# Two instruction groups change places on TensorE and three on VectorE in a batch loop

## The reference

```python
qx = _ln(_fp8_linear_pertensor(ln_out, wqx, ...).reshape(b, s, g, hpg, d), qxln_w, qxln_b)
kvx = einsum('bsi,oi->bso', cond, w_kv_x)          # cond: the context, 8 x 512 x 256
kx, vx = split(kvx, 2, axis=-1)
kx = _ln(kx.reshape(b, sc, g, d), kxln_w, kxln_b)
xout = softmax(einsum(qx, kx) * scale) @ vx
catq = _div_clamp_fp8(concat([core, xout]), proj_smooth)
x = x + einsum(catq, wproj) * (proj_in_scale * proj_w_scale)
```

## Time and profile before

| what | us |
|---|---|
| median of 3 runs | 427.75 (425.83 to 428.95) |
| the profiled execution's own time | 427.4 |
| its span in the trace | 425.6 |
| busy: PE, DVE, ACT, POOL | 414.7, 347.2, 248.8, 35.8 |

### The profile page before, as it was taken

One profiled execution on the slowest core, in us unless ns is written; L12 is line 12 of the kernel. 1 busy time (PEld: TensorE's weight loads), 2 busy tenths in 40 slices (PEclk: granted clock), 3 DMA queues, 4 the chain that ended last, 5 costly groups with the idle time before them and its releaser, 6 DMA issues.

```text
span 425.6 us, 6868 instructions
## 1 busy us (share of the span) xinstructions
PE 414.7 (97%) x2427; PEld 292.2 (69%) x2433; DVE 347.2 (82%) x699; ACT 248.8 (58%) x780; POOL 35.8 (8%) x58
## 2 busy tenths in 40 slices
PE   8999999999999999999999999999999999999897
PEld 3453455788885767778676686785486799837596
DVE  5889999987999899689899998978887787746831
ACT  2478898688547777748986677664505263220220
POOL 0010000040000001100001000010010004101000
PEclk9999999999999999999999999999999999999999
DMA  7599120500002015993554835688337979730000
GB/s 240 226 191 415 39 85 2 199 2 26 27 2 99 1 51 123 201 306 78 132 124 92 198 70 108 155 187 359 74 78 246 390 267 241 151 125 2 2 2 25
DMA packets 14591, 56.80 MB, mean 133 GB/s; under 512 B 1824, under 2 KB 2912, under 8 KB 13280
## 3 DMA queue, kind: packets, MB, share of 16 engines
q1 hardware_dynamic: 11104, 39.31, 25.3%
q0 software_dynamic: 3456, 17.11, 21.4%
HBM read 41.40 MB, written 0.26 MB: 98 GB/s over the span
## 4 chain that ended last, share of the span: by engine, by line
PE 74%; DVE 12%; issue 6%; DMA 4%; ACT 3%; POOL 1%; SPq 0%; DVEq 0%; ACTq 0%; POOLq 0%
PE PS L482 11%; PE PS L1817 10%; PE PS L453 8%; PE PS L454 8%; PE PS L455 8%; PE PS L1846 3%; PE PS L535 3%; PE PS L1287 3%; DMA lutw_dt.float<-luttmp_dt.float 2%; PE PS L1832 2%; DMA raw_dt.float<-in_wk_nat 1%; PE PS L492 1%; PE PS L1153 1%; PE PS L1135 1%; PE PS L1295 1%
## 5 line engine op out<-in xcount | busy, mean ns | idle before, releaser
L605 ACT ACTIVATE sq_dt.float<-PS 128x128 bf16<-128x128 f32 x256 | 67.0, 279 | 27.0 <-PE PS L455 20.5
L482 PE MATMUL PS<-s_dt.float,ctx_ring_dt.float 128*128 128x512 f32 x128 | 57.8, 593 | 0.0
L605 ACT ACTIVATION_READ_ACCUMULATOR sq_dt.float<-PS 128x1 f32 x256 | 53.6, 210 | 0.0
L453 PE MATMUL PS<-wkc_dt.float32r,ctx_hi_dt.float32r 128*128 128x512 f32 x128 | 51.5, 402 | 0.1
L454 PE MATMUL PS<-wkT_dt.float32r,ctx_hi_dt.float32r 128*128 128x512 f32 x128 | 50.0, 390 | 0.0
L455 PE MATMUL PS<-wkc_dt.float32r,ctxT_ring_dt.float32r 128*128 128x512 f32 x128 | 49.9, 390 | 0.0
L687 ACT ACTIVATE luttmp_dt.float<-low_bit_dt.float,vec_dt.float,small_dt.float 128x1536 f32<-128x1536 uint8 x24 | 38.5, 1654 | 8.5 <-DMA lutw_dt.float<-luttmp_dt.float 8.5
L1817 PE MATMUL PS<-wch_dt.float,xs_dt.float 128*128 128x512 f32 x96 | 42.0, 592 | 0.0
L482 PEld LDWEIGHTS PS<-s_dt.float,ctx_ring_dt.float 128*128 128x128 f32 x128 | 23.6, 190 | 23.6 <-issue 23.0
L700 POOL DMA_DIRECT2D lutw_dt.float<-luttmp_dt.float x21 | 18.2, 869 | 234.7 <-DVE luttmp_dt.float L694 234.7
L694 DVE SCALAR_TENSOR_TENSOR luttmp_dt.float<-idx_dt.float,luttmp_dt.float 128x1536 f32<-128x1536 uint8 x21 | 36.6, 1753 | 0.0
(11 more groups left out here) (304 smaller groups left out, 851.3 us busy)
## 6 DMA issues: line engine op xcount, KB each, us to landing
lutw_dt.float<-luttmp_dt.float POOLq DMA_DIRECT2D x21, 768.0 KB, 6.1
wch_dt.float<-in_chunks SPq DMA_DIRECT2D x5, 1024.0 KB, 7.9
ctxT_ring_dt.float<-in_ctxT SPq DMA_DIRECT2D x8, 512.0 KB, 3.4
ctx_ring_dt.float<-in_ctx SPq DMA_DIRECT2D x8, 512.0 KB, 3.9
keysT_dt.float<-in_ctxT SPq DMA_DIRECT2D x8, 512.0 KB, 7.0
keys_dt.float<-in_ctx SPq DMA_DIRECT2D x8, 512.0 KB, 8.0
zu_dt.float<-in_wproj SPq DMA_DIRECT2D x1, 2048.0 KB, 7.2
A_first_dt.float<-in_wproj SPq DMA_DIRECT2D x1, 2048.0 KB, 10.2
```

What stands on the lines that cost most here:

```text
L453: nc.tensor.matmul(o, x_hi, hi[:, c, :], start=c == 0, stop=False)
L482: last = nc.tensor.matmul(mix_bank(b, c), keysr[k][:, t, c * 128:c * 128 + 128], sS[k][:, t, :], start=t == 0, stop=t == KT - 1)
L605: last = nc.scalar.activation(sq[:, (4 * hf + g) * D:(4 * hf + g + 1) * D], key_bank(b, 2 * t + hf)[:, g * D:(g + 1) * D], ACT.Square, acc ...
```

## The change

`total` and `spread` change places on TensorE in the steps 1 to 6. On VectorE `sums` goes ahead of `lo_of_A` (steps 2 to 6; in step 1 `lo_of_A` was behind both already), and the first table term goes from ahead of `shift` to behind `normalise` (steps 1 to 6). Item 7's code is not changed.

```diff
@@ TensorE, step
                 maxima(b)
                 if prev and more:
                     mix(b - 1, 1 - k, 1)
+                    spread(b)
                     total(b - 1)
-                    spread(b)
@@ VectorE, step
+                sums(b - 1, 1 - k)
                 if b > 1:
                     lo_of_A(dve, b + 1)
-                sums(b - 1, 1 - k)
                 maxima(b)
                 if b == 1:
                     lo_of_A(dve, 2)
-                term(dve, b - 1, 0)
                 shift(b, k)
                 normalise(b - 1, 1 - k)
+                term(dve, b - 1, 0)
```

## The result

| | before | the change |
|---|---|---|
| median, 8 runs each in one comparison | 426.87 us (425.83 to 428.95) | 429.70 us (429.00 to 431.13) |
| profiled execution | 427.4 us, span 425.6 | 429.0 us, span 427.2 |

The ratio is 1.0064, 95% interval 1.0044 to 1.0084: slower by 0.6%, which the repeated runs can tell from no change, and within the 1% of the prediction. Forecast were 429.8 us and a loss of 2.05 us.

What follows compares the result with a forecast made beforehand. TensorE's order of work was taken to bound the six changed steps. +1.25 us (step 1) and +0.8 us (step 4) make +2.05 us, 429.8 us against the median 427.75; range 427.0 to 432.0 us, 8 times in 10.

Steps and rivals of the forecast that it cites:

- Step 1: TensorE waits for late maxima before the spread, and its third key product waits through total and ScalarE: +1.25 us.
- Step 4: VectorE has no idle time behind the shift, so TensorE's fourth score product waits 1.35 instead of 0.54 us: +0.8 us.
- The exchange in the other steps: Spread ahead of total on TensorE where maxima are early: zero cost, covered by the mix with 1.09 us margin.
- the sums: Sums ahead of A's low part on VectorE: only margin, maxima about 0.85 us earlier in step 4; no gain in time.
- the normalisation's tie: VectorE's normalisation against ScalarE's Exp of the inverse: margin shrinks from 1.37 to about 0.1 us, priced at nothing.
- The later DMAs: The first term's accumulating DMA, on POOL's queue, is issued some 5 to 6 us later: taken as zero cost.
- The clock: TensorE's clock was forecast to stay 1.00; rival: it falls to 1.2 GHz in step 1, 441.2 us, chance 0.03.
- at most 0.66 us: TensorE's idle time in steps 1 and 4, taken as all a better order could give; faster rival 427.1 us, chance 0.07.
- Steps 3 and 5 are free: VectorE's 0.81 us of lateness fits into idle times of 0.65 and 0.47 us (step 5: 0.63 and 0.46): no cost.
- if a light step grows: Sign that the forecast is wrong: steps 2, 3, 5 and 6 were to stay as long as before.
- VectorE's idle time before each shift: Sign in the changed profile: VectorE idle 1.6 to 1.7 us before each shift.
- The rival of the late leaf: Step 3's third leaf waits for its DMA, delaying the normalisation; at most 2.1 us reach TensorE, 431.9 us; chance 0.15.

Runs made afterwards that it cites:

- the reordering on ScalarE: The change, with ScalarE's split of the context moved ahead of the inverse: 428.40 us, ratio 1.0027 to before.
- The last kernel: Against the change: total ahead of spread in step 1, term in its old place, ScalarE's context split ahead of the inverse; 426.68 us, ratio 0.9980 to before.
- The kernel with the term back in step 4 alone: The change, with total ahead of spread in step 1 and the term ahead of shift in step 4 only: 426.29 us, ratio 0.9982 to before.

## Why the prediction was right

*The sum.* Step 1: forecast +1.25, measured +1.22, and in the two pieces of it that the forecast named: TensorE idle before the spread (0.59 us, released by VectorE's last maxima instruction), and the third key product held through ScalarE. The exchange alone reproduced it, its removal in step 1 took it away, and the reordering on ScalarE took away the part that was said to run through ScalarE. Step 4: forecast +0.8, measured +0.80, wait forecast 1.35 us and measured 1.35 us. The term was its cause, and taking the term back in this step alone gave all of it back.

*Where luck helped.* That 429.8 us came so close to the measured 429.70 is in part luck. The sum stood on a median of 427.75 us from three executions of before, and eight gave 426.87; by medians the loss is 2.8 us (interval 1.9 to 3.6), where 2.05 was forecast. What the forecast got right is its 2.05 against the 2.11 us of the six steps.

*What was priced at nothing.* The exchange in the other steps, the sums and the normalisation's tie were free. The later DMAs cost nothing either: the longest took 11.6 us to land instead of 9.7, and the leaf of step 5 waited 2.00 us instead of 1.98. The clock stayed at 1.00 in every stretch of the profiled execution, over two gaps of 0.6 us in step 1 and one of 1.35 us in step 4. The section on HAM oscillation of "TensorE: Matmul & The Clock Gate" in the Trainium skill tells of a matmul stream that lost the full clock at each of its long waits for a DMA. The gaps here are shorter than the waits of that case, so it did not say that this change would come out worse than the sum, as the forecast read it; that a gap as long as there costs the clock, no run here shows.

*What was sized wrong without harm.* The forecast said that a better order could give back at most 0.66 us, TensorE's visible idle time. The last kernel gave back 1.03 us in the same six steps, since a wait costs more than the gap that the trace shows (last section). It also said that a measurement cannot tell 1% from no change; the executions told the change (0.6%) and five of the eight kernels of the experiments (0.2 to 0.6%) from the kernel before.

*What was missed without harm.* "Steps 3 and 5 are free" came out right by less than was said. I counted 0.81 us of lateness against idle times of 0.65 and 0.47 us. But an earlier shift brings VectorE to the multiplications of the normalisation before TensorE has done the value products that still read their target, a wait that the profile before does not show:

```profile
192.01 1.29 DVE L867 TENSOR_TENSOR px_dt.float<-PS,vecs_dt.float 128x512 f32<-128x512 f32 x2 [0.91 <-PE PS L535]
...
204.99 0.18 DVE L828 TENSOR_SCALAR small_dt.float<-small_dt.float 128x32 f32<-128x32 f32 x1
205.21 0.20 DVE L830 TENSOR_TENSOR small_dt.float<-small_dt.float 128x32 f32<-128x32 f32 x1
...
205.89 1.29 DVE L739 TENSOR_TENSOR s_dt.float<-PS,small_dt.float 128x512 f32<-128x512 f32 x2
```

So in step 3 the whole earlier shift is given back, VectorE has no idle time left before the key scale where the earlier trace rows show 0.65 and 0.47 us, and its first tile is scaled at about 205.89 + 0.69 = 206.58. TensorE starts the product that needs it at 206.73, and its weight load has already begun to wait for the tile:

```profile
206.64 0.19 PEld L453 LDWEIGHTS PS<-A_hi_dt.float32r,ctx_hi_dt.float32r 128*128 128x128 f32 x1 [0.17 <-DVE s_dt.float L739]
```

The step grew by 0.04 us, and step 5 by 0.06 us. They grew by the same amounts with the term alone, and by 0.02 us at most with the exchange alone. So the room was used up; by an estimate from these rows another 0.2 us of lateness would have been paid nearly in full, twice. Taken strictly, the sign "if a light step grows" had begun to show. The code names this wait (`v_full` in `normalise`), and the forecast should have followed the shift to it.

*What was named wrong in the signs.* VectorE's idle time before each shift was to be 1.6 to 1.7 us; it is 1.73 and 1.72 us in steps 2 and 3, but 1.26 us in steps 4 to 6, because VectorE enters them late, and nothing in step 1, where the low part of A lies between. The start of the shift is set by the spread, so this changed no step's length. The rival of the late leaf had its cause, but not its effect: the last leaf of step 3 waited for its DMA, by 0.19 us where the rival needed 2.8.

```profile
184.10 1.67 ACT L687 ACTIVATE luttmp_dt.float<-low_bit_dt.float,vec_dt.float,small_dt.float 128x1536 f32<-128x1536 uint8 x1 [0.19 <-DMA lutw_dt.float<-luttmp_dt.float]
```

*Median against loop.* The ratio says +1.9 to +3.6 us, the loops say +2.11, within it. The ratios of all eight kernels of the experiments hold their loop's difference too (+1.13 in 0.4 to 1.7, +1.77 in 1.6 to 3.5, -0.82 in -1.4 to 0.0, and so on).

## What to carry to other kernels

Before two instructions change places in a saturated engine's queue, ask for each step of the loop which of their inputs comes last; the exchange that is free in five steps can cost in the one where the earlier instruction covered the later one's wait, and the price is that of everything that runs through the delayed one, not of the gap that it leaves. Filler work belongs where its engine waits anyway: moved behind the wait, it costs its whole length in the one step that has no idle time. And an earlier start is worth something only as far as the next wait behind it.

## What the runs showed of the hardware

A wait of TensorE costs more than the idle time that the trace shows before the waiting matmul. Step 4 lasts 24.99 us without a wait, 25.82 with 0.54 us of it, 26.62 with 1.35 and 27.46 with 2.20: each time 0.27 to 0.29 us more than the wait. The kernel with the term back in step 4 alone shows where this lies, at the same product:

```profile
229.63 0.39 PE L458 MATMUL PS<-A_dt.float32r,ctx_hi_dt.float32r 128*128 x1
229.86 0.39 PE L459 MATMUL PS<-A_hi_dt.float32r,ctxT_ring_dt.float32r 128*128 128x512 f32 x1
230.23 0.50 PE L457 MATMUL PS<-A_hi_dt.float32r,ctx_hi_dt.float32r 128*128 128x512 f32 x1
230.56 0.40 PE L458 MATMUL PS<-A_dt.float32r,ctx_hi_dt.float32r 128*128 x1
```

In a stream of these matmuls one starts about 0.23 us after the other, while each is shown 0.39 us long, so a wait can cost 0.16 us before a gap shows. Here the product starts 0.37 us after its forerunner, 0.14 us late without a gap. And the first matmul after a wait is 0.50 us long, with the next start 0.33 us after it, another 0.10 us. The two make 0.24 of the 0.25 us that this step is longer than 24.99. At this product a new wait thus costs about 0.28 us above its visible gap, and one that only grows does not pay that again. At the spread of step 1 it was less: 0.56 us were visible and the step was 0.74 us longer. The forecasts of steps 1 and 4 survived this because the products that set the time there, the third key product and the fourth score product, had a wait already.

The granted clock is not quite the same in all executions of a kernel. Its mean over the span was 1.00 in five of the change's eight (median 429.49 us) and 0.996 in three (430.77 us). Of the term alone it was under 1.00 in seven of twelve (431.00 against 428.19 us). Of before it was 0.996 in 5 of the 35 executions of one comparison (428.19 us, against 427.41 at 1.00) and in 8 of the 33 of the other (428.28 us, against 427.13). So the term alone lies 0.8 us above before where both have 1.00, on five executions of it, and the upper end of its ratio comes from the others. The two other kernels with all terms behind the normalisation show a lower clock in 2 of 12 and 1 of 10 executions. In none of the ten profiled executions does the clock fall before the last matmul has ended, so where it falls in the others, and whether the term's move makes it more frequent, stays open.
